# Four-layer decoder on one core: layer 1's two attentions in one chain of eight batches, layer 0's context stage in 18 phases with an order per engine, and the last attention's rows turned earlier

## What is computed

```python
x = x + L0_attn(layernorm(x))
xq = fp8_round_1x128(layernorm(x)); x = x + einsum(xq, fp8_round_128x128(ctx))      # layer 0, context
h = relu(layernorm(x) @ ternary(c_fc)) ** 2                                          # layer 0, feed-forward
h = round(h / rowmax(h) * 255) / 255 * rowmax(h);  x = x + h @ ternary(c_proj)
x = x + causal_attention_16_heads(layernorm(x), w_q, w_k, w_v) @ w_o                 # layer 1, self
q = int8_rows(layernorm(x)) @ int8(wq).T + bq;  k, v = split(ctx @ wkv.T + bkv)      # layer 1, context
x = x + int8_rows(attention_16_heads(q, k, v)) @ int8(wp).T + bp
...                                                                                  # layers 1 (ffn), 2, 3
core, xout = attention(ln(q), ln(k), v), attention(ln(qx), ln(kx), vx)               # layer 3
x = x + fp8(concat(core, xout) / smooth) @ wproj.T * scale
```

## Time and profile before

| | us |
|---|---|
| median of 3 runs (2461.18 to 2463.77) | 2462.4 |
| the profiled execution, its own time | 2461.4 |
| its span in the trace | 2459.6 |
| layer 0's context stage, DVE's first tile to the stage's end | 335.0 to 436.5 |
| layer 1, self-attention stage | 436.5 to 600.8 |
| layer 1, cross-attention stage | 600.8 to 791.2 |
| last attention: preparation, and from its first scores to its end | 1593.3 to 1630.5 to 2237.8 |

### The profile page before, as it was taken

The page is one execution under the profiler, slowest core; times in us unless marked ns, Lnnn a source line. Parts: engine busy times, 40 slices in busy tenths (PEclk is TensorE's granted clock), DMA queues, the critical chain, the costliest instruction groups (busy, mean ns, idle before and its releaser), DMA issues. The chain is left out here.

```text
span 2459.6 us, 38364 instructions
## 1 busy us (share of the span) xinstructions
PE 2058.6 (84%) x13521; PEld 1469.2 (60%) x13521; DVE 1605.5 (65%) x4116; ACT 1120.4 (46%) x2539; POOL 873.9 (36%) x1388
## 2 busy tenths in 40 slices
PE   6999955897797579986469899869999999997991
PEld 4888833564563245644145576547878777785671
DVE  4867568345465835555757788868888888875333
ACT  2356633232342924434565756335555555552330
POOL 3248843112011311111100000046766667764444
PEclk9999978897997679987579999989999999998996
DMA  6124420000000030000000000041111111106543
GB/s 252 44 84 138 152 90 1 1 2 1 1 1 28 0 149 1 1 2 37 1 0 1 1 1 1 20 159 40 44 40 52 44 40 41 54 26 225 116 138 103
DMA packets 57693, 130.96 MB, mean 53 GB/s; under 512 B 6656, under 2 KB 23552, under 8 KB 55520
## 3 DMA queue, kind: packets, MB, share of 16 engines
q1 hardware_dynamic: 52656, 115.80, 13.8%
q0 software_dynamic: 4560, 12.46, 2.4%
q10 hardware_dynamic: 288, 0.26, 0.0%
HBM read 100.31 MB, written 26.08 MB: 51 GB/s over the span
## 5 line engine op out<-in xcount | busy, mean ns | idle before, releaser
L1269 ACT ACTIVATE K<-ps 128x768 f32<-128x768 f32 (+1 forms) x128 | 110.5, 864 | 164.2 <-PE ps L1085 162.4
L2190 DVE TENSOR_TENSOR_SCAN W<-W,ps 128x512 f32<-128x512 f32 x128 | 155.8, 1217 | 43.3 <-issue 25.3
L2791 POOL TENSOR_TENSOR K<-K 128x512 f32<-128x512 f32 x128 | 134.4, 1050 | 137.9 <-DVE K L2588 137.9
L2142 PEld LDWEIGHTS ps<-K 128*128 128x128 f32 x1024 | 139.3, 199 | 64.6 <-issue 51.8
L2731 ACT ACTIVATE K<-ps,K 128x256 f32<-128x256 f32 x128 | 60.6, 474 | 243.4 <-DVE K L2572 243.4
L2583 DVE TENSOR_SCALAR K<-ps,K 128x128 f32<-128x128 f32 x384 | 130.9, 403 | 34.9 <-POOL K L2808 34.5
L2142 PE MATMUL ps<-K 128*128 128x128 f32 x1024 | 141.5, 283 | 6.8 <-DVE W L2190 6.8
L1307 POOL CAST K<-K 128x8 bf16<-128x8 f32 x64 | 14.6, 229 | 365.9 <-issue 207.5
L2777 POOL TENSOR_SCALAR K<-K 128x1 f32<-128x1 f32 x16 | 3.6, 224 | 375.9 <-DVE K L2638 373.0
L2161 PE MATMUL ps<-W,C 128*128 128x512 f32 x256 | 133.1, 602 | 0.7 <-DVE W L2198 0.6
L237 POOL TENSOR_SCALAR Z<-Z 128x1 f32<-128x1 f32 x80 | 19.2, 241 | 321.4 <-DVE Z L232 321.4
(11 more groups left out here) (530 smaller groups left out, 5829.8 us busy)
## 6 DMA issues: line engine op xcount, KB each, us to landing
W<-split_weights SPq DMA_DIRECT2D x32, 768.0 KB, 4.4
split_weights<-W SPq DMA_DIRECT2D x40, 384.0 KB, 2.6
W<-in_m SPq DMA_DIRECT2D x32, 256.0 KB, 4.8
results<-K SPq DMA_DIRECT2D x63, 128.0 KB, 2.5
W<-split_weights SPq DMA_DIRECT2D x1, 5376.0 KB, 17.0
W<-in_wproj SPq DMA_DIRECT2D x16, 256.0 KB, 3.0
W<-in_m SPq DMA_DIRECT2D x32, 128.0 KB, 5.3
W<-split_weights SPq DMA_DIRECT2D x1, 3072.0 KB, 20.5
```

Of the source, the lines that this page charges most:

```text
L1269: e.activation(to, made, ACT.Exp, scale=self.SCALE).then_inc(*self.up("exp"))
L2142: m = e.matmul(ps[1 + 2 * (n % 2)][:, b * 128:(b + 1) * 128], self.dtuT[h][:, i, b * 128:(b + 1) * 128], self.diag[s % 4][:, b * 128:(b + ...
L2190: e.tensor_tensor_scan(self.st[i % 3], self.a[i % 3], ps[1 + 2 * (i % 2)][:, :], 0.0, ALU.mult, ALU.add).then_inc(*sig.up("m scan"))
L2791: e.tensor_tensor(Pv, Pv, st[:, 4:6].unsqueeze(2).to_broadcast([128, 2, 256]), ALU.mult).then_inc(*sig.up("x scaled"))
```

## The change

It has three parts. Line numbers in the diff's functions are those of the changed kernel.

**Layer 0's context stage.** 18 phases, and for each engine a tuple that gives the order of the phases inside a step. The product, the ACT copy and the split stand in phases of their own (2, 6, 7), two or more steps apart from what they need. The square goes from POOL to ACT (phase 9, line 913), and the rounding from one DVE pass to two ACT passes (phase 11, lines 917 and 920).

**Layer 1.** `L1Attn` and `L1Cross` become one stage, `L1Heads`, with 8 batches (32 units): batches 0 to 3 causal, 4 to 7 not. Quantising a tile's normalised row now follows its norm inside the chain (`apply_next`), the bias is added per tile (`pool_after`), and the turned row is kept through the "norm" step in bank 7. There is no preparation ahead of the cross-attention's units any more.

**The last attention.** `LEAD` is 6 instead of 5, a tile's norm preparation takes 4 steps instead of 5, and the feed-forward turns stand 5 and 9 steps after their start instead of 5 and 6. First step -25 instead of -26: 160 steps.

```diff
 class L0Cross:
-    PHASES = 14
+    PHASES = 18
+    PE = (17, 13, 12, 8, 6, 2, 1)
+    DVE = (14, 7, 3, 10, 16, 15, 5, 4, 0)
+    ACT = (11, 9, 17, 12, 8, 6, 1)
+    POOL = (15, 4)
...
-    def steps(self):
+    def steps(self, order):
         for step in range(NT + self.PHASES - 1):
-            for t in range(max(0, step - self.PHASES + 1), min(NT, step + 1)):
-                yield t, step - t
+            for ph in order:
+                if 0 <= step - ph < NT:
+                    yield step - ph, ph
...
-                v.step(e.tensor_scalar(R, R, m[:, 1:2], 255.0, ALU.mult, ALU.mult).then_inc(v.own, 1))
-                v.wait_ge(v.own, v.n)
-                v.wait_ge(sig["l0f rows turned"], i - 2)
-                e.tensor_scalar(Q, R, RND, RND, ALU.add, ALU.subtract).then_inc(*sig.up("l0f rows"))
-            elif ph == 9:
+                e.tensor_scalar(R, R, m[:, 1:2], 255.0, ALU.mult, ALU.mult).then_inc(*sig.up("l0f on scale"))
+            elif ph == 14:
...
+            elif ph == 9:
+                R = self.rr[i % 4]
+                a.wait_ge(sig["relu"], 2 * i + 2)
+                e.activation(R, R, ACT.Square).then_inc(*sig.up("squares"))
+            elif ph == 11:
+                R = self.rr[i % 4]
+                a.wait_ge(sig["l0f on scale"], i + 1)
+                a.step(e.activation(R, R, ACT.Identity, bias=g.rnd).then_inc(a.own, 1))
+                a.wait_ge(a.own, a.n)
+                a.wait_ge(sig["l0f rows turned"], i - 2)
+                e.activation(self.rq[i % 3], R, ACT.Identity, bias=g.back_rnd).then_inc(*sig.up("l0f rows"))
...
-            elif ph == 6:
-                R = self.rr[i % 4]
-                p.wait_ge(sig["relu"], 2 * i + 2)
-                e.tensor_tensor(R, R, R, ALU.mult).then_inc(*sig.up("squares"))
...
-class L1Attn(SmallHeads):
-    PER, VHEADS, DV, CAUSAL, QUANT, NEXT, WO, PREPARED, SETS, MROWS = 16, 16, 16, True, False, 4, "wo1", 0, 3, 1
-class L1Cross(SmallHeads):
-    PER, VHEADS, DV, CAUSAL, QUANT, NEXT, WO, PREPARED, SETS, MROWS = 16, 16, 16, False, True, 5, "wp1x", 1, 3, 1
+class L1Heads(SmallHeads):
+    PER, VHEADS, DV, PREPARED, SETS, MROWS, NB, CAUSAL = 16, 16, 16, 0, 3, 1, 2 * B, False
...
+    def causal(self, b):
+        return b < B
+    def after(self, tile):
+        return (self.g.norms[4], tile) if tile < NT else (self.g.norms[5], tile - NT)
...
+    def apply_next(self, v, tile):
+        nx, i = self.after(tile)
+        if tile >= NT:
+            return nx.apply(v, i)
...
+        v.step(v.e.tensor_scalar(to, self.g.x(i), nx.mv[:, i, 0:1], nx.rs[:, i, :], ALU.subtract, ALU.mult).then_inc(v.own, 1))
+        v.wait_ge(v.own, v.n)
+        chain_int8_rows(v, to, to, *(self.ax[:, i, c:c + 1] for c in range(3)), self.sig.up(nx.name + " xn"))
+    def pool_after(self, p, tile):
...
+        p.e.tensor_tensor(self.g.x(i), self.g.x(i), self.g.p("bp1"), ALU.add).then_inc(*self.up("biased"))
...
 class L3Cross:
-    FIRST, LEAD, N = -26, 5, 128
-    PREP, FFN = (-26, 0, 32, 64), (94, 101, 108)
+    FIRST, LEAD, N = -25, 6, 128
+    PREP, FFN = (-25, 0, 32, 64), (94, 102, 110)
...
-            order += [("prep", b, ph // 5) for b, ph in self.at(self.PREP, s, 10) if ph % 5 == 3]
-            order += [("ffn", b, ph - 5) for b, ph in self.at(self.FFN, s, 7) if ph >= 5]
-            if 0 <= s + 3 < self.N and (s + 3) % 4 != 3:
-                order.append(("rows", *divmod(s + 3, 4)))
+            order += [("prep", b, ph // 4) for b, ph in self.at(self.PREP, s, 8) if ph % 4 == 3]
+            order += [("ffn", b, (ph - 5) // 4) for b, ph in self.at(self.FFN, s, 10) if ph in (5, 9)]
+            u = s + self.LEAD - 2
+            if 0 <= u < self.N and u % 4 != 3:
+                order.append(("rows", *divmod(u, 4)))
...
-STAGES = [(1, L0Attn), (3, L0Cross), (4, L1Attn), (5, L1Cross), (6, L1Ffn), (7, L2Attn), (8, L2Cross), (9, L2Moe),
+STAGES = [(1, L0Attn), (3, L0Cross), (5, L1Heads), (6, L1Ffn), (7, L2Attn), (8, L2Cross), (9, L2Moe),
```

342 lines of the change are left out of this document (166 added, 176 removed).

## The result

| | before | changed |
|---|---|---|
| median of the runs, us | 2463.1 (4) | 2396.6 (2388.2 to 2400.9, 4) |
| profiled execution, its own time | 2461.4 | 2393.9 |
| context stage | 104.7 | 90.6 |
| layer 1's attentions | 354.8 | 311.1 |
| last attention | 648.8 | 642.9 |

The ratio is 0.972 (95% interval 0.968 to 0.976): the changed kernel is faster. The profiled executions lie 67.5 us apart, where 52.1 were forecast. Times the 2462.4 us of the forecast the ratio gives 2393.2 us, just under the range of 2394 to 2430; the median itself, 2396.6, is 2.6 us above the range's lower end.

The account below looks back on a forecast made before the run. DVE was taken to bound the context stage, a half-idle PE stretch to cost layer 1, PE's waits the last attention. 11.5 + 38.6 + 2 = 52.1 us off 2462.4 gave 2410 us, range 2394 to 2430.

Parts of the forecast that it names:

- The terms for DVE's list: Context stage: rounding 5.6, stretched first rounding operation 4.9 and scale pass 2.4 us go, so DVE's 80.5 us become 67.6.
- DVE is the bound: Layer 0's context stage: DVE, busy 80.5 of 101.5 us, was taken as what limits the stage.
- The forecast's 90 us: Context stage after the change: ACT's long work from about 28 to 82 us, 6 of tail, 90 with waits.
- The four batches: Layer 1, exponentials 23 to 55: one batch at 33.7 and three at 34.6 us, 137.6 instead of 181.2.
- The handoffs: Layer 1: passing the cross-attention's norm through the units gives back 5 us, 3.5 of them sure as 8 x 0.44.
- The 7.6 us at the scores: Last attention: rows turned one step earlier, so the scores' waits for copied rows, 7.6 us, go.
- the wait at a turn: Last attention: all 12 norm turns wait for ACT's copy, 1.3 us each, 15.6 us against 11.1 before.
- the end step: Last attention: one more step at the end has no projection to cover its waits, 0.7 us lost.
- the clock stays up at the end: Rival, 14 in 100: the cross-attention's last nine exponentials take 23 us instead of 30.3, whole 2403 us.
- ACT or the clock as the context stage's bound: Rival, 18 in 100: ACT's steps wait for PE at the low clock, stage 97 or 98 us, whole 2418.
- Norm's handoffs in bank 7: Rival, 12 in 100: DVE's string shows in full in layer 1's chain, 20 us given back instead of 5, 2425.
- The slower case: Rival, 3 in 100: in layer 1 a late quantised row costs up to 8.4 us a tile, 67 us, 2473.

Follow-up runs that it names:

- order_square_first: Changed kernel with the square back on POOL, first in its step, and the rounding back on DVE, 18 phases kept: context stage 90.1 us, median 2391.7 us.
- round_on_dve: Changed kernel with the rounding alone back on DVE, one pass for ACT's two: context stage 86.7 us, median 2387.5 us.
- norm_turned_three_times: Changed kernel with the two PE turns of each causal tile's quantised row made three times: exponentials 23 to 55 in 139.4 us, median 2402.3 us.
- three strings: Changed kernel with DVE's five quantising operations of each causal tile made three times: exponentials 23 to 55 in 160.2 us, median 2424.7 us.

## Why the prediction was right or wrong

The result lies just outside the range because every part won more than forecast (2.6, 5.1 and 4.0 us) and the unchanged stages 3.8 more. Part 2 alone passed its own bound, 43.7 us for at most 40.

**Part 1, 11.5 forecast, 14.1 won: size near, reason wrong.** The terms for DVE's list came out (67.8 us for 67.6, the scale pass 0.75), and ACT's list was 50.6 for 54. The step that failed is the one from the list to the stage: "DVE is the bound", so each microsecond off its list is one off the stage. Before, DVE was idle 21.2 of 104.7 us; the orders alone take that to 9.2 with the list 2.6 us shorter, and win 14.6. The moves take 12.4 us from the list, and lose 16 without the orders. With them the square's move wins 3.4 us and the rounding's, a term of 5.6 us won in the forecast, loses 2.6 (1 to 2 if the clock is allowed for), 0.8 in all.

The forecast's 90 us were then added up along ACT: 28 us until its long work, 54 of list, 6 of tail, 2 of waits. On the same measure, from DVE's first tile, the changed kernel has 26.2, 53.2 and 8.0, 87.4 us. That the middle was right is luck: it is as long with ACT's list of 27.7 us in order_square_first (53.5), and only some 3 us shorter with one of 35.0 in round_on_dve (50.4). So ACT's list alone didn't set it either. The page of the Trainium skill weighed there ("Perfetto Trace Analysis", Optimizing Scalar/DVE Operations) has the condition that DVE be saturated; I took 80.5 of 101.5 us as meeting it. For the rounding, which is better on DVE, the page's rule was the better guide, and my reading of its condition the fault.

**Part 2, 38.6 forecast, 43.7 won.** The chain was right and its length from 23 to 55 was 5.8 us too long, in two terms. The four batches were set at 33.7 + 3 x 34.6 = 137.6. The second of them, which begins with the last causal unit, took 34.3 us with its two handoffs and so belongs to the causal pace; the last is one in which the projections end, and takes 32.9 us as its counterpart before did (exponentials 15 to 23 of the cross-attention): 33.7 + 33.7 + 34.6 + 32.9 = 134.9. The handoffs were set at 5 and came to 1.9 here. Of these 5 us 3.5 were called sure, 8 turned tiles at 0.44 us, and this floor made the bound of 40 (43.6 - 3.5). It is the step that failed: the 0.44 us are what the rows of a pair of turns span, not what they take from PE, which norm_turned_three_times puts at 0.22 us; and two of the eight tiles stand ahead of number 23. Outside that distance 2.3 us are given back ahead of number 23, where the projections and two handoffs now stand, and 1.6 won at the end by the clock. 44.4 - 2.3 + 1.6 = 43.7.

**Part 3, 2 forecast, 6.0 won.** The 7.6 us at the scores went, as said. The mis-sized term is the wait at a turn: 1.3 us taken, 0.87 measured at ten of twelve, the lower bound. That makes 11.3 instead of 15.6 and the charge 0.2 instead of 4.5; the end step and waits that moved take the rest. By its own terms the part's ends were 7.2 won and 1.2 lost, not the 6 and 5 stated.

**The rest.** 3.8 us of the 67.5 are scatter. The clock's part of the rival "the clock stays up at the end" came in between: 0.82 in the first run and 28.6 us for 30.3, 25.6 or 24.1 in others. The Trainium skill ("TensorE: Matmul & The Clock Gate", Part 1) has it that the gate isn't tied to a place in the program; the same instructions at 0.77 and 0.93 above agree.

**The other rivals.** ACT or the clock as the context stage's bound: not as forecast, but the stage does follow the clock, 90.7 us at PEclk 0.71 to 0.74, 89.3 at 0.77, 87.5 at 0.79, with DVE and ACT as busy in all. Norm's handoffs in bank 7: no. The slower case had the right kind (DVE's string in a unit's way) and the wrong point: lateness of the row has 9.8 us of room (525.05 to 534.85) and costs nothing when that shrinks to 1, but the string's length has only about 0.7 us beyond its 1.6, where 7 were given. With three strings the chain is 32.4 us longer, part of it by the clock, and the kernel still on the faster side.

## What to carry to other kernels

An engine busy 80% of a stage isn't its bound until its waits have been priced against the order of its list: here reordering won 14.6 us, moving work off the engine without reordering lost 16, and the shortest stage, 84.6 us, has the orders, the square's move and half of the rounding's. Before a pass leaves an engine for a slower one, try the order with the pass where it is, and each pass by itself: of the two moved here one won and one lost. The rows of two turns overlap, so a row's length isn't its price. And a string put into this full pipeline was nearly free up to the slack of the next instruction behind it; beyond that PE waited, and in some batches the clock fell as well: double such a string once to learn how near that point is.
